# One table load for all conditioning weights, copied on the chip by GpSimd and ScalarE, with two reorderings on VectorE

## The reference: what is computed

```python
W = weights[condition]                        # 64 batches, 16 tables of 64 x 64
y = einsum('bct,bcd->bdt', x, W)              # x: 64 x 64 x 1024
base = einsum('bsi,oi->bso', y, W_org)        # 1024 x 1024
q = einsum('bi,ki->bk', y.mean(axis=1), Wq)
scores = einsum('bk,ek->be', q, lora_keys) / sqrt(K)
coeffs = softmax(scores, axis=-1)             # 8 experts
h = einsum('bsi,eir->bser', y, lora_down)     # 8 x 1024 x 64
delta = einsum('be,bser,ero->bso', coeffs, h, lora_up)
out = x + base + delta
```

## Time and profile before

| | |
|---|---|
| median of three runs | 714.96 us (714.73 to 715.47) |
| the profiled execution | 714.7 us, its span 712.9 us |
| TensorE clock granted | 1.00 of full speed, the whole span |
| TensorE busy | 701.1 us, 98% |
| VectorE busy | 505.9 us, 71% |
| ScalarE busy | 286.5 us, 40% |
| GpSimd busy | 118.2 us, 17% |
| DMA | 138.6 MB, mean 194 GB/s |

### The profile page before, as it was taken

How to read it: one execution, slowest core, us unless ns; L and a number is a source line. 1 busy time by engine, 2 the same in 40 slices (tenths; PEclk the granted TensorE clock), 3 DMA queues, 4 the chain that set the end, 5 groups by cost and what they waited for, 6 DMA issues and landing times.

```text
span 712.9 us, 10677 instructions
## 1 busy us (share of the span) xinstructions
PE 701.1 (98%) x3345; PEld 587.1 (82%) x3345; DVE 505.9 (71%) x821; ACT 286.5 (40%) x580; POOL 118.2 (17%) x108
## 2 busy tenths in 40 slices
PE   8999999999999999999999999999999999999997
PEld 7877787888888888888888878888888888888876
DVE  3888687585784864655656997786777677776774
ACT  4456665856666742443524822221122222211220
POOL 2210000000000000000000033323332333333360
PEclk9999999999999999999999999999999999999999
DMA  8987376484684754423443846666676776766732
GB/s 240 280 260 232 106 231 209 145 255 149 192 244 149 207 194 128 137 104 90 135 160 121 316 136 194 221 214 219 219 235 237 236 236 220 233 203 213 268 119 88
DMA packets 100986, 138.60 MB, mean 194 GB/s; under 512 B 18874, under 2 KB 70082, under 8 KB 98114
## 3 DMA queue, kind: packets, MB, share of 16 engines
q1 hardware_dynamic: 100592, 137.85, 60.0%
q10 hardware_dynamic: 338, 0.07, 0.0%
HBM read 82.32 MB, written 55.57 MB: 193 GB/s over the span
## 4 chain that ended last, share of the span: by engine, by line
PE 87%; DVE 6%; issue 4%; DMA 1%; SPq 1%; ACT 1%; POOL 0%; DVEq 0%; ACTq 0%; POOLq 0%
PE x_ps L1456 23%; PE w_ps L1456 17%; PE x_ps L1378 11%; PE h_ps L1378 11%; PE x_ps L1412 11%; PE w_ps L1412 8%; PE y_ps L1337 6%; DVE tb_l L873 1%; DVE tu_l L873 1%; DVE blk L876 1%; DMA t_dram<-st 1%; DVE up_raw L873 1%; DVE ysum L889 1%; DMA cw_sb<-in_L_cond_weights_dram 0%; DVE ba_l L873 0%
## 5 line engine op out<-in xcount | busy, mean ns | idle before, releaser
L566 POOL TENSOR_TENSOR blk<-blk,blkx 128x512 f32<-128x512 f32 x60 | 93.1, 1552 | 276.3 <-DMA blkx<-in_x_dram 160.4
L876 DVE TENSOR_TENSOR blk<-w_ps,blk 128x512 f32<-128x512 f32 x96 | 66.1, 688 | 68.1 <-PE w_ps L1412 32.4
L1456 PE MATMUL x_ps<-tb_h,ba_h 128*128 128x512 f32 x256 | 100.0, 390 | 0.8 <-DVE ba_l L873 0.4
L1456 PE MATMUL x_ps<-tb_l,ba_h 128*128 128x512 f32 x256 | 99.6, 389 | 0.0
L1456 PE MATMUL x_ps<-tb_h,ba_l 128*128 128x512 f32 x256 | 99.6, 389 | 0.0
L602 ACT ACTIVATE ba_h<-bs 128x512 fp32r<-128x512 f32 x64 | 38.1, 626 | 125.7 <-DVE bs L873 125.7
L1456 PE MATMUL w_ps<-tb_h,ba_h 128*128 128x512 f32 x192 | 74.9, 390 | 0.0
L1456 PE MATMUL w_ps<-tb_h,ba_l 128*128 128x512 f32 x192 | 74.7, 389 | 0.0
L1456 PE MATMUL w_ps<-tb_l,ba_h 128*128 128x512 f32 x192 | 74.7, 389 | 0.0
L602 ACT ACTIVATE ba_h<-yb 128x512 fp32r<-128x512 f32 x48 | 28.4, 621 | 101.9 <-DMA yb<-y_dram 101.9
L876 DVE TENSOR_TENSOR blk<-x_ps,blk 128x512 f32<-128x512 f32 x64 | 42.5, 683 | 34.2 <-PE x_ps L1456 34.2
(11 more groups left out here) (100 smaller groups left out, 1407.8 us busy)
## 6 DMA issues: line engine op xcount, KB each, us to landing
x_sb<-in_x_dram SPq DMA_DIRECT2D x32, 512.0 KB, 4.3
y_dram<-y_full SPq DMA_DIRECT2D x64, 256.0 KB, 3.1
yb<-y_dram SPq DMA_DIRECT2D x32, 512.0 KB, 7.3
out_dram<-blk SPq DMA_DIRECT2D x64, 256.0 KB, 3.9
blkx<-in_x_dram SPq DMA_DIRECT2D x30, 512.0 KB, 6.8
r_dram<-blk SPq DMA_DIRECT2D x56, 256.0 KB, 2.5
blk<-r_dram SPq DMA_DIRECT2D x14, 1024.0 KB, 6.7
t_dram<-st SPq DMA_DIRECT2D x16, 448.0 KB, 4.3
```

The lines of the kernel that those rows point to most:

```text
L566: pool.tensor_tensor(blk[p % 3][:, b, :], blk[p % 3][:, b, :], blkx[:, h, n, :], ALU.add).then_inc(x_added, 1)
L876: nc.vector.tensor_tensor(dst, a, b, ALU.add).then_inc(done, 1)
L1456: mm = nc.tensor.matmul(bank, ba[s][n][:, k, :], tb[w][n][:, k, :], start=(first and k == 0 and i == 0), stop=(k == 3 and i == 2), skip_gr ...
```

## The change

All 16 tables are loaded once, as `table` (64 partitions, 16 x 64), by one DMA that stands behind the first half of x0; x1 to x3 and the rest follow on the same queue. Each tile's two 64 x 64 blocks are copied from `table` into `cws` with a register as index: on GpSimd for all tiles but 2 and 3, on ScalarE for those two. SyncE no longer reads table numbers or loads rows, and x5 to x7, the up pieces and the y stores stand in another order. To make room, `yg` lies on the place of two of the `gs` sums, and `gate_sums` waits for their readers.

On VectorE the low parts of the half tiles 0, 2, 4 and 6 come straight from PSUM ahead of the copies; in the rounds from the second on, the low parts of the last two half tiles go ahead of the y sums and the gate product; the up part P5 is split behind P3. `make_y(5)` stands behind the first product's three passes.

```diff
@@ memory
-        cw_sb = small("cw_sb", [P, 4, BT, C])
+        table = small("table", [C, NCOND, C])
-        yg = small("yg", [P, BQ, E, KC])
+        yg = at("yg", 178176, [P, BQ, E, KC])
+        def cw_count(t):
+            return BT * (t if t < 2 else t - 2)
+        def table_of(which):
+            return table[:, :, :].rearrange("c n (d h) -> c n h d", h=2)[:, bass.ds(which, 1), :, :]
@@ SyncE
-            load_x(0)
-            load_x(1)
-            sp.wait_ge(cond_loaded, 16)
-            sp.wait_ge(first_steps, 1)
...
+            sp.dma_start(x_sb[:, 0, 0:4 * P], x_v[0, :, 0:4 * P]).then_inc(x_loaded[0], 16)
+            sp.dma_start(table[:, :, :], table_v).then_inc(table_loaded, 16)
+            sp.dma_start(x_sb[:, 0, 4 * P:8 * P], x_v[0, :, 4 * P:8 * P]).then_inc(x_rest_loaded, 16)
+            for t in range(1, 4):
+                load_x(t)
             load_down_half(0, 0, down_loaded[0])
...
             load_x(5)
-            load_cw(5)
+            store_y(2)
+            store_y(3)
             load_up(0)
             load_up(1)
-            store_y(2)
-            store_y(3)
+            load_x(6)
             load_up(2)
             load_up(3)
-            for n in range(4, 8):
-                store_y(n)
-            for t in (6, 7):
-                load_x(t)
-                load_cw(t)
+            store_y(4)
+            store_y(5)
+            load_x(7)
+            store_y(6)
+            store_y(7)
...
                         load_x(t + 4 + m)
-                        load_cw(t + 4 + m)
@@ GpSimd
-            def turn_cw(t):
+            def turn_cw(t, rows):
-                i = t % 4
-                pool.wait_ge(cw_loaded[i], 16 * BT * (t // 4 + 1))
                 if t >= 3:
                     pool.wait_ge(y_done, tile_made(t - 3))
-                pool.tensor_copy(cws[:, t % 3, :, :, :],
-                                 cw_sb[:, i, :, :].rearrange("p b (d h) -> p b h d", h=2)).then_inc(cw_ready, 1)
+                for b in range(BT):
+                    pool.wait_ge(cw_ready, cw_count(t) + b)
+                    pool.tensor_copy(cws[b * C:(b + 1) * C, t % 3, b:b + 1, :, :], table_of(rows[b])).then_inc(cw_ready, 1)
...
-            turn_cw(0)
-            turn_cw(1)
-            turn_cw(2)
-            turn_cw(3)
+            turn_cw(0, rows_0)
+            turn_cw(1, rows_1)
+            rows_4 = rows_of(4)
+            rows_5 = rows_of(5)
+            pool.wait_ge(cw_ready, cw_count(4))
+            turn_cw(4, rows_4)
+            pool.wait_ge(cw_ready, cw_count(5))
             for t in range(3):
                 split_y(t)
-            turn_cw(4)
+            pool.wait_ge(y_lo[1], 3)
+            turn_cw(5, rows_5)
+            pool.wait_ge(cw_ready, cw_count(6))
             split_y(3)
@@ ScalarE
+            act.wait_ge(table_loaded, 16)
+            turn_cw(2, rows_2)
             split_y(0)
+            act.wait_ge(y_done, tile_made(0))
+            turn_cw(3, rows_3)
             copy_y(1)
...
-                if q == 0:
-                    split_up(P5, 1)
+                if 1 <= q <= 4:
+                    spread_w(2 * q - 1, 1)
+                hi_block(j0, P1, 0, 0)
+                hi_sum(j0, P7, 2)
+                if q == 0:
                     act.wait_ge(up_loaded[2], 16)
                     act.wait_ge(up_loaded[3], 16)
                     split_up(P2, 0)
                     split_up(P3, 0)
+                    split_up(P5, 1)
@@ VectorE
                 dve.wait_ge(y_summed, 8 * q + 8)
+                if q >= 1:
+                    for n in (P5, P6):
+                        dve.wait_ge(ga_hi[n], 2 * q)
+                        dve.wait_ge(ga_lo[n], 2 * q)
+                    dve.wait_ge(s_ready[3], 2 * q)
...
-            copy_y(0)
             split_y(0)
-            copy_y(2)
+            copy_y(0)
             split_y(2)
-            copy_y(4)
             split_y(4)
-            copy_y(6)
             split_y(6)
             split_down_half(0, 0)
+            copy_y(2)
             split_down_half(1, 0)
+            copy_y(4)
+            copy_y(6)
...
+                if q > 0:
+                    split_y(n - 3)
+                    split_y(n - 1)
                 if q == 1:
                     for m in range(2, 8):
                         sum_y(8 + m)
                 gate_sums(q)
                 if q == 0:
                     split_down(2)
-                if q > 0:
-                    split_y(n - 3)
-                    split_y(n - 1)
                 split_z(q)
...
-                    split_up(P5, 2)
...
-                    split_up(P2, 3)
-                    split_up(P3, 4)
+                    split_up(P2, 2)
+                    split_up(P3, 3)
+                    split_up(P5, 4)
                     split_up(P7, 5)
@@ TensorE
-                pe.wait_ge(cw_ready, t + 1)
+                if n == 1:
+                    pe.wait_ge(x_rest_loaded, 16)
+                if t in (2, 3):
+                    pe.wait_ge(cw_by_act, BT * (t - 1))
+                else:
+                    pe.wait_ge(cw_ready, cw_count(t) + BT)
...
                             if i == 1:
-                                make_y(5)
                                 pe.wait_ge(y_lo[0], 4)
...
+                        make_y(5)
                         continue
```

More of the change, by code:

```diff
@@ L164, in adaln_ffn @@
         x_loaded = [sem(f"x_loaded_{i}") for i in range(4)]
-        cw_loaded = [sem(f"cw_loaded_{i}") for i in range(4)]
+        table_loaded = sem("table_loaded")
+        x_rest_loaded = sem("x_rest_loaded")
         down_loaded = [sem(f"down_loaded_{n}") for n in range(DP)]
@@ L182, in adaln_ffn @@
         cw_ready = sem("cw_ready")
+        cw_by_act = sem("cw_by_act")
         first_steps = sem("first_steps")
@@ L430, in _ @@
             load_x(4)
-            load_cw(4)
             store_y(0)
@@ L602, in copy, with rows_of, turn_cw @@
                 nc.scalar.activation(dst, src, ACT.Copy).then_inc(done, 1)
-            def row(t):
-                return act.value_load(cond_sb[0:1, BT * t + 1:BT * t + 2], min_val=0, max_val=NCOND - 1)
-            def load_row(t, which):
-                act.dma_start(cw_sb[C:2 * C, t, 1, :], cond_w[which, :, :]).then_inc(cw_loaded[t], 16)
+            def rows_of(t):
+                return [act.value_load(cond_sb[0:1, BT * t + b:BT * t + b + 1], min_val=0, max_val=NCOND - 1)
+                        for b in range(BT)]
+            def turn_cw(t, rows):
+                for b in range(BT):
+                    copy(cws[b * C:(b + 1) * C, t % 3, b:b + 1, :, :], table_of(rows[b]), cw_by_act)
             def copy_y(n):
@@ L1424, in up_2 @@
                     pe.wait_ge(c11_ready, j)
-                up_product(j, P2, w_ps[:, 0, :], True, 3)
+                up_product(j, P2, w_ps[:, 0, :], True, 2)
             def up_6(j):
```

66 lines of the change are left out of this document (25 added, 41 removed).

## The result

The changed kernel takes 710.65 us (median of 6 runs, 709.78 to 711.87) against 714.93 for the kernel before on the same chip (6 runs, 714.4 to 715.79): the ratio is 0.9941, with a 95% interval of 0.9928 to 0.9953. The forecast was 709.7, 5.25 less; the interval says 3.4 to 5.1 less. The profiled execution has a span of 709.0 us against 712.9, 3.9 less.

What follows compares the result with a forecast made beforehand. TensorE, busy 98% of the span, bounds the kernel, so only its gaps before 110 us can be won: 3.1 + 1.1 + 0.45 + 0.2 + 0.4 = 5.25 off 714.96 gives 709.7 us; own range 708.9 to 710.7, 8-in-10 range 706.9 to 713.2.

Steps and rivals of the forecast that it cites:

- Table and hand-out: Kernel start: `cws` 0 ready at 5.8, first y stays at 6.68; nothing won, nothing lost below 0.9 us more.
- The front, 3.1: Six half tiles and first product's passes: the run of 12 products starts at 17.0 instead of 20.08, 3.1 us won.
- The rival of a late front: Start: x3 at 12.4, slow GpSimd copies or blocked splits; 12 products at 18.6, 1.5 won, total 711.3; chance 0.22.
- Down and y parts beside GpSimd: VectorE beside GpSimd's splits: only operations with two SBUF inputs slow down; if copies count too, total 0.4 less.
- Tile 6, 1.1: y matmuls of tile 6 near 41: no DMA for `cws`, x6 loaded earlier, so TensorE's wait goes; 1.1 us won.
- Up pieces, 0.45: First round's up products: reordered splits put VectorE 4.6 earlier, TensorE no longer waits at 59.27; 0.45 us won.
- Two low parts ahead of the y sums, 0.2: Second round: TensorE's 1.5 wait near 79 goes, z comes 1.3 later, P2 waits 1.3; 0.2 us won.
- z costs nothing: Rival, second round: TensorE's wait for P2 does not come, 1.3 more won, total 708.4; chance 0.15.
- `st` store, 0.4: SyncE near 110: the store of `st` goes out at least 1.7 earlier, TensorE's wait at 109.68 goes; 0.4 us won.
- 110 us and on: From 110 us: nothing won or lost, the long stretch stays 288 of 288 busy, no gap after 110.
- The front is won and lost again at the up products: Rival: up pieces land at 41.5, second scalings at 48.8, only 0.4 earlier than before; total 714.0; chance 0.08.
- Slower, up pieces starve: Rival: up pieces starve behind x6, landing at 45, second scalings at 52.3, 3.1 later; total 717.5; chance 0.07.

Runs made afterwards that it cites:

- table_twice: The changed kernel with the table's transfer made twice, first into a place nobody reads, the hand-out waiting for the second load alone; 711.22 us, 0.9946.
- x_halves: On top of sums_split: x1 to x3 loaded in halves, the second halves of x2 and x3 behind first halves of two down pieces; 707.63 us, 0.9897.
- old_start: The changed kernel, table kept, with VectorE's old start: copies first, low parts from the copies, y of half tile 5 later; 710.81 us, 0.9933.
- before_plus: The kernel before plus VectorE's new start, y of half tile 5 behind the passes, and x6 with its rows ahead of up pieces 2 and 3; 714.78 us, 0.9995.
- before_up6: The kernel before, old start kept, with P5 split behind P3 and x6 with its rows ahead of the last two up pieces; 712.83 us, 0.9969.
- z_behind: The changed kernel with the last two low parts of y again behind the y sums, gate product and z, from the second round on; 709.76 us, 0.9914.
- up_ahead: On top of sums_split: up pieces 0 and 1 loaded ahead of the y stores of half tiles 2 and 3; 708.43 us, 0.9903.
- both: x_halves and up_ahead together, with the three y sums moved as in sums_split; 707.37 us, 0.989.
- last_wait: On top of both: in the first round one 0.42 us VectorE sum moved from ahead of the second scalings to behind P4's low part; 706.88 us, 0.9889.
- old_up: The changed kernel with the up part P5 split ahead of P2 and P3 again, and ScalarE's splits ahead of the high parts; 712.01 us, 0.9955.
- sums_split: The changed kernel with three of the six y sums moved from the second round's start to the first round's end on VectorE; 708.71 us, 0.9895.
- before_all: The kernel before with all parts of the change but the table and the order of z; 712.32 us, 0.9962.

## Why the prediction was right, and where it was off

The time came out 1.0 us above the forecast, at the upper edge of its own range (708.9 to 710.7), by the forecast's own mechanism: the gaps before 110 us close, the long stretch gains and loses nothing, TensorE stays the bound. By the spans the miss is larger, 1.35 (3.9 won of 5.25), and there was luck inside the sum: two of its errors had opposite signs, as the second point tells, and terms were added that are not independent. By steps:

- **Table and hand-out**: right. `cws` 0 at 6.5 instead of 5.8, first y at 6.62 (6.7 forecast). table_twice shows the slack put at 0.9: a hand-out 1.0 later cost nothing further on.
- **The front, 3.1**: measured 2.5, the mis-sized term. The step that failed is "2.1 MB at the 347 of whole rows make 7.1 us, so x3 lands at 10.2". x3 was there at about 11.3: 2.36 MB in the 8.15 us from the forecast's own start (0.75 + 2.4) is 290 GB/s, between its 253 and 347. The fourth and fifth half tiles made (4 and 6) wait for x; x_halves removes just that and no half tile waits. But 290 is no constant of the ring either, since table_twice has x3 as early with 0.26 MB more in front. A second reading was wrong the other way: the forecast took the duration of 16 y records, 2.1, for two half tiles, where their starts stand 1.79 apart (x_halves; 25.50 to 27.28 in the kernel before, where it wasn't shown). Six half tiles take 5.4 instead of 6.2, so without waits the fifth would start at 10.3, not 10.75, and x3, even landing at 10.2, had next to no slack. The rival of a late front had x3 at 12.4 and the 12 products at 18.6; the measured 11.3 and 17.56 lie between the two. VectorE's order, forecast from its row durations, is worth 1.0 at the 12 products but only 0.3 to 0.4 by 110 us (old_start), because it runs into VectorE's chain. Fronts of one kernel also differ between executions, 17.06 to 17.56 for the same code in five kernels, so the miss of 0.6 is only partly a miss of the sum.
- **Down and y parts beside GpSimd**: right by the row. The Trainium skill (SBUF — State Buffer, "Who interferes with whom") names the operations of VectorE that take the port pair shared with GpSimd; this trace agrees for the one with two SBUF inputs (`down_l`: 1.72 us beside GpSimd's splits, 0.68 at 13.88 just before them) and shows no such hold for a 128x512 f32 copy from PSUM, 0.68 at 16.73. The 0.4 that the rule could have cost did not come.
- **Tile 6, 1.1**: 1.3, right. But it is worth that only with the up pieces reordered: without that it gave nothing, even together with a front 0.6 earlier (before_plus). The forecast added the two as if independent; in this change they stood together, so the sum was safe here.
- **Up pieces, 0.45**: -0.3, wrong in what is left. The forecast said that VectorE's chain from scores to second scalings shrinks by 1.6, from 16.1, to 14.5, and that TensorE then never waits. It is 15.14, with 0.75 us of waits. 14.5 is right where the pieces are there and the scores are later: 14.42 in old_start and 14.43 in before_up6, with no wait above 0.15 us in the up products. In the changed kernel two things are in the way. The first is the landing: ScalarE waits 1.63 for the first up piece, which stands behind y stores on the queue. The forecast had seen the landing of the last pieces as a risk ("gives back at most 0.5") but left it out of its sum. z_behind, the same code up to here, waited only 0.43, so about 0.35 of the 0.75 belongs to this execution. The second is the rest, 0.40 to 0.44, which stays in z_behind, x_halves, up_ahead and both: after the earlier front VectorE comes to the scores 0.14 later behind TensorE's matmul (0.40 instead of 0.26) and its chain is 0.24 longer than in old_start; why it is longer was not traced. That last_wait removes it by taking 0.42 us of work off VectorE (13.87, no wait) shows VectorE to be what TensorE waited for. The reorder itself works (old_up: chain 16.56, 1.95 us of waits instead of 0.75).
- **Two low parts ahead of the y sums, 0.2**: 0.0. By the spacing the old wait was worth 1.7, not 1.5, and the new ones take as much. The mechanism is as forecast down to the row (no gap near 75, ScalarE idle for z 3.14 instead of 1.88, a wait at the third up product), with a second small wait of 0.46 at 80.05 that was not. z_behind and sums_split show that one late z makes both. The rival "z costs nothing" is out. Three of six sums in VectorE's idle time would have won both waits.
- **`st` store, 0.4**: 0.5, right, and made by 110 us. **110 us and on**: right, 284.00 of 284.00.
- **The front is won and lost again at the up products**: this rival's mechanism is real. It takes all in before_plus and, in the changed kernel, 0.7 of the 1.0 that VectorE's order wins.
- **Slower, up pieces starve**: the mechanism is there at 1.6 us on ScalarE, far from the 5 us from which it would have decided.

What stays open: why x3 and the up pieces land about a microsecond apart in different executions and kernels, and how the 1.7 to 2 of the table divide between the early hand-out of tiles 1 to 3, the earlier `st` store and the small loads that are gone.

## What to carry to other kernels

An earlier load or removed wait counts only if the next chain on the slower helper engine moves with it: before adding such terms, write down that chain's length (here VectorE's 14 to 16 us from scores to scalings) and see who is early at its end. Here 1.0 won at the front was worth 0.3 behind that chain, and 2.0 were worth nothing where the chain was longer. Putting urgent work ahead of a producer's other work moves the wait to what depends on the delayed part; moving that other work into the producer's idle time removes it. Where many loads stand on one queue from the start, their order and size matter: load what the first consumer reads, in its size. A landing computed from bytes and the best rate in the profile was 1.1 early here, and bytes in front alone do not give it; leave a margin of about a microsecond. Take the price of a run of matmuls from the spacing of their starts, not from their durations.

## What the runs showed of the hardware

A wait of TensorE can be followed by a low clock and then costs more than itself. In before_plus, with waits of 1.15 and 0.70 at 9.41 and 11.24, the granted clock from 12 to 20 us is 0.80, and 16 y matmuls take 3.19 instead of 1.95:

```profile
12.00:20.00 8.00, 7.98 (x42) 7.23 (x42) 5.51 (x8) 4.13 (x8) 2.99 (x2) 0.80 1.03 274
```

In before_all, after the 2.25 above, it is 0.63 from 77.5 to 82 and 0.50 from 79.2 to 81.8, the 1.2 GHz level, where products stand 0.43 apart instead of 0.227. Its lead over the kernel before falls from 1.65 to 0.05 us between 77.5 and 82.2. That waits like these are enough is not shown: the kernel before waits 0.67 and 1.32 at the same place of the front and 1.48 at 79.17, before_up6 1.56 and 0.37, all at 1.00. The changed kernel is at 1.00 in both stretches shown.

Issuing takes longer when more is still on its way. SyncE's eight issues of the down pieces took 4.45 us before, begun at 8.72; in the changed kernel they begin at 4.08, with the table and the x tiles still on their way, and take 8.75. That the queue was full is the likely reason, and not shown. An `up_raw` load is 8.4 us from issue to landing (median of four; 5.8 before):

```profile
4.08 8.75 SPq L406 DMA_DIRECT2D down_raw<-in_L_ffn_lora_down_dram  x8
```
```profile
up_raw<-in_L_ffn_lora_up_dram SPq DMA_DIRECT2D x4, 512.0 KB, 8.4
```
